# Kernel of four residual layers: rows of 528 columns instead of 514 for the split inputs of both convs

## The reference

```python
x = x + conv(x, W0, groups=4, taps=9, pad=4) + context + bias      # layer 0
x = x + agg_w1[b] @ x + agg_b1[b]                                  # layer 1
x = x + agg_w2[b] @ x + agg_b2[b]                                  # layer 2
x = x + conv(x, W3, groups=4, taps=9, pad=4) + context + bias      # layer 3
```

## Time and profile before

| | |
|---|---|
| median of 3 runs | 2578.09 us (2578.03 to 2578.33) |
| the profiled execution | 2577.78 us |
| its span, from the first to the last instruction | 2575.7 us |
| PE busy | 2550.1 us (99%), 11068 matmuls |
| weight loads (PEld, beside PE) | 2069.8 us (80%) |
| ACT busy | 2100.5 us (82%) |
| DVE busy | 1955.4 us (76%) |
| POOL busy | 16.1 us (1%) |
| DMA, mean over the span | 314 GB/s |
| granted TensorE clock, mean | 0.997 |

### The profile page before, as it was taken

The page is one execution under the profiler, slowest core; times in us unless marked ns, Lnnn a source line. Parts: engine busy times, 40 slices in busy tenths (PEclk is TensorE's granted clock), DMA queues, the critical chain, the costliest instruction groups (busy, mean ns, idle before and its releaser), DMA issues.

```text
span 2575.7 us, 42996 instructions
## 1 busy us (share of the span) xinstructions
PE 2550.1 (99%) x11068; PEld 2069.8 (80%) x11068; DVE 1955.4 (76%) x5032; ACT 2100.5 (82%) x1937; POOL 16.1 (1%) x29
## 2 busy tenths in 40 slices
PE   8999999999999999999999999999999999999998
PEld 6888888888888888888888888888888888888886
DVE  8777777777777777777777777777777777777774
ACT  6888888888888888888888888888888888888885
POOL 2000000000000000000000000000000000000000
PEclk9999999999999999999999999999999999999999
DMA  7888888888888888888888888888888888888876
GB/s 254 316 320 317 318 319 319 315 318 323 318 312 321 323 318 313 320 324 316 315 320 323 315 317 319 322 317 316 320 320 317 317 319 319 316 318 322 317 297 237
DMA packets 334986, 809.31 MB, mean 314 GB/s; under 512 B 37370, under 2 KB 39426, under 8 KB 302210
## 3 DMA queue, kind: packets, MB, share of 16 engines
q1 hardware_dynamic: 332736, 807.69, 84.3%
q10 hardware_dynamic: 2242, 1.53, 0.2%
HBM read 137.97 MB, written 134.23 MB: 106 GB/s over the span
## 4 chain that ended last, share of the span: by engine, by line
PE 98%; DMA 1%; DVE 1%; ACT 0%; SPq 0%; issue 0%; DVEq 0%; ACTq 0%
PE pair L877 82%; PE quad L927 14%; PE pair L917 1%; DMA x_ch<-x_ph 0%; DVE partial L701 0%; DMA mix<-att_saved 0%; DMA x_ph<-in_small 0%; SPq L269 0%; SPq L321 0%; SPq L294 0%; DMA att_saved<-att 0%; ACT x_out L569 0%; ACT x_ch L422 0%; DVE x_hi L734 0%; ACT x_ph L575 0%
## 5 line engine op out<-in xcount | busy, mean ns | idle before, releaser
L877 PE MATMUL pair<-x_hi,w_hi 128*128 128x512 f32 x3072 | 1227.7, 400 | 2.9 <-DVE x_lo L752 1.2
L877 PE MATMUL pair<-x_hi,w_lo 128*128 128x512 f32 x3072 | 1213.5, 395 | 0.0
L877 PE MATMUL pair<-x_lo,w_hi 128*128 128x512 f32 x3072 | 1209.2, 394 | 0.0
L877 PEld LDWEIGHTS pair<-x_hi,w_lo 128*128 128x128 f32 x3072 | 579.7, 189 | 137.5
L877 PEld LDWEIGHTS pair<-x_lo,w_hi 128*128 128x128 f32 x3072 | 582.0, 189 | 131.7
L877 PEld LDWEIGHTS pair<-x_hi,w_hi 128*128 128x128 f32 x3072 | 579.0, 188 | 131.3 <-DVE x_lo L752 1.6
L484 ACT ACTIVATE x_ph<-pair,bias_now 128x512 f32<-128x512 f32 x512 | 351.2, 686 | 254.8 <-PE pair L877 254.7
L422 ACT COPY x_ch<-x_in 128x1024 f32<-128x1024 f32 x255 | 528.3, 2072 | 0.0
L475 ACT COPY x_out<-x_ch 128x1024 f32<-128x1024 f32 x252 | 517.3, 2053 | 0.0
L493 ACT ACTIVATE x_ph<-pair,bias_now 128x512 f32<-128x512 f32 x508 | 355.5, 700 | 191.3 <-PE pair L877 191.3
L734 DVE CAST x_hi<-x_ch 128x512 fp32r<-128x512 f32 x512 | 204.9, 421 | 325.9 <-DMA x_ch<-x_ph 325.9
(11 more groups left out here) (83 smaller groups left out, 772.9 us busy)
## 6 DMA issues: line engine op xcount, KB each, us to landing
x_ph<-x_ch SPq DMA_DIRECT2D x1024, 256.0 KB, 2.5
x_ch<-x_ph SPq DMA_DIRECT2D x1024, 256.0 KB, 2.6
x_in<-in_x SPq DMA_DIRECT2D x128, 1024.0 KB, 5.6
out<-x_out SPq DMA_DIRECT2D x128, 1024.0 KB, 4.3
x_out<-in_W SPq DMA_DIRECT2D x8, 144.0 KB, 3.9
expert<-in_e ACTq DMA_DIRECT2D x2, 512.0 KB, 8.1
mix<-att_saved SPq DMA_DIRECT2D x2, 512.0 KB, 6.3
x_ph<-in_small ACTq DMA_DIRECT2D x1, 458.5 KB, 3.4
```

The source lines that it names most:

```text
L877: mm = nc.tensor.matmul(conv_bank[g % 2], w[l][:, m, g, :], x[:, g, m:m + N], start=(m == 0 and x is hi and w is w_hi), stop=(m == BLK - 1 ...
```

## The change

The rows of the four split inputs of the convs get 14 more columns, which nothing reads or writes. `ROW` = 512 + 16 = 528 columns are 2112 bytes, 33 x 64. The slices that are written and read keep their columns. Each of the four tensors grows from 8224 to 8448 bytes per partition, so x_lo begins at byte 57728 (902 x 64), x3_hi at 115328 (1802 x 64) and x3_lo at 123776 (1934 x 64); the tensors between x_lo and x3_hi stand 448 bytes further on, and those behind x3_lo 896 bytes. x_hi stays where it was. The instructions of every engine, their order and their waits are the same before and after, but for the addresses.

```diff
@@ -38,6 +38,7 @@
     HALO = BLK // 2
+    ROW = N + 16
     K = a["e0"].shape[0]
@@ -65,16 +66,16 @@
         x_ph = sb("x_ph", [C, G, N])
-        x_hi = sb("x_hi", [C, G, N + 2 * HALO], f32r)
-        x_lo = sb("x_lo", [C, G, N + 2 * HALO], f32r)
+        x_hi = sb("x_hi", [C, G, ROW], f32r)
+        x_lo = sb("x_lo", [C, G, ROW], f32r)
...
         x3_ph = sb("x3_ph", [C, G, N])
-        x3_hi = sb("x3_hi", [C, G, N + 2 * HALO], f32r)
-        x3_lo = sb("x3_lo", [C, G, N + 2 * HALO], f32r)
+        x3_hi = sb("x3_hi", [C, G, ROW], f32r)
+        x3_lo = sb("x3_lo", [C, G, ROW], f32r)
```

## The result

The changed kernel takes 2585.85 us in the median of 8 runs (2584.46 to 2587.25), the kernel before 2577.39 us in as many (2576.72 to 2578.33). The ratio is 1.0032, with a 95% interval of 1.0023 to 1.0042: 8.5 us slower. The forecast was 2586.4 us.

The account below looks back on a forecast made before the run. TensorE's back-to-back matmuls were taken to bound the kernel. 2577.8 - 0.2 (64 bytes) + 8.5 (16 bytes) = 2586.1 us, with 0.3 for the median 2586.4; range 2572 to 2594.

Parts of the forecast that it names:

- What bounds the kernel: Whole kernel: TensorE, busy 2550.1 of 2575.7 us; other engines matter only if they become late.
- the cover of conv4's first matmul: The third x1 group is evacuated 0.57 us before conv4, which waits for it, begins; cost 0.
- The 16 bytes: Conv matmuls, m = 1 of groups 1 and 3: offset 12 becomes 4, 0.017 us a triple, 512 triples, 8.5 us slower.
- The 64 bytes: Conv matmuls: starts at multiples of 64 go from 3 to 12 per 36, worth only 0.2 us.
- The other terms: VectorE and ScalarE work, tensors moved by 448 or 896 bytes, waits and halo fills: 0 in all.
- Rival 2: Timing depends on more of the address than its last 16 bytes, new places quick: 2563 or 2570 us; chance 0.12.
- Rival 1: Conv matmuls: the start does not matter, the pattern belongs to banks or weights; 2578 us, chance 0.31.
- Rivals 3 and 4: Conv starts beside 64 cost 19.3 ns each, 2534 us, chance 0.03; or conv4 waits for late moves, 2591 us, chance 0.03.

Follow-up runs that it names:

- the pitch alone: Rows of 528 columns, with 200 spare columns behind each split tensor keeping places modulo 1024 bytes, against the kernel before: 2584.47 us, ratio 1.0026.
- two columns on: The changed kernel with the data two columns further on in each row of 528: 2564.32 us, ratio 0.9951 to the kernel before.
- The kernel with one start per block: No layers: 2528 matmuls in blocks of 16, each block with one moving and one weight start, while x is copied; sixteen starts take 3.63 to 3.78 us.

## Why the prediction came out

**What bounds the kernel** was right: in the loop of none of these kernels does PE wait for another engine, and the cover of conv4's first matmul is still there, 0.58 us.

**The 16 bytes** were the right step, and most of the convs' time came from it: m = 1 of the odd groups went from 0.69 us to between 0.70 and 0.72. Forecast were 0.067 us a batch. At just these four triples the changed kernel takes 0.076 us more and the pitch alone 0.072, so this term was right in place and in size. What it left out is that the other places move too: in sum they cost 0.03 us more in the changed kernel, where the convs lose 0.11 in all, and 0.02 less with the pitch alone, where they lose 0.05; over many places it is 0.07. Also right was to trust the offset and not the PSUM bank: the same groups in the same banks speed up and slow down with the data's column, and with rows of 576 columns both banks show one pattern.

**The 64 bytes** buy nothing, as said; with not one start at 64, two columns on is 21 us quicker than the changed kernel. The argument for it was not sound, though. The middle product was taken as a yardstick for an aligned row, 232.5 ns, but it stood at a slow distance from its weights, and at a good one takes 2.72 / 12 = 226.7 ns.

**The other terms** hold the error, and two of the signs that the prediction named did not come: the conv piece was to be 16.82 us and is 16.86, the middle was to stay at 2.79 and fell to 2.74. Moving tensors by multiples of 64 was priced at 0. It gave the middle 0.05 us a batch, some 6 us of gain in all, and the convs some 0.05 of loss beyond what the pitch alone costs; the two nearly cancel. Had they had one sign, the forecast would have missed by more than 10 us. That the total came within 1 us is in this part luck. Rival 2 named this dependence (more of the address than its last 16 bytes) and expected it to be a gain; it was one for the middle only. Rival 1's time did not come, but the weights, which it named, do have a part in the pattern. Rivals 3 and 4 did not happen.

**What stays open.** Why 12 should be the cheapest offset and 4 the dearest is not explained; nor is how one spacing follows from the last ones in a changing sequence. The two effects were measured, not derived.

## What to carry to other kernels

Where TensorE's fp32r matmuls are back to back and nothing else is late, look at the starts in the trace by their place in the loop before touching a layout: here a fixed pattern of some nanoseconds came from addresses and not from contention. Aligning rows is no aim by itself; here the quicker layouts of the convs begin at 8, 12 and 0 bytes within 16, at both places of the weights that were tried, and the middle product, whose rows keep one start, is quickest with the weights at the same place modulo 256 bytes as the row. Change pitch and places apart, since padding one tensor moves all that follow, and their effects can hide each other.

## What was not expected of the hardware

A stream of equal matmuls is not evenly spaced: after some matmuls it mostly repeats a short pattern, and where that has one to three members its mean is 16, 18.7, 20, 21.3, 24, 26.7, 28, 29.3 or 32 cycles above 256, so that its sum is a multiple of 8 cycles of 1.2 GHz. The best, 226.7 ns for 512 columns, was never undercut in a block's steady state. The spacing seems to have a memory: conv1's changed when only the rows of the product before it were moved, and one distance can end in either of two patterns. Load of the DMA engines does not show in it. The kernel with one start per block meets distances 0 and 12 again behind the end of its copy, and takes 3.63 and 3.67 us there, as against 3.63 and 3.66 with the DMA engines at work (stretch, us, busy, granted clock, DMA share, GB/s):

```profile
549.73:553.36 3.63, 3.63 (x18) 1.00 0.00 0
586.96:590.63 3.67, 3.67 (x18) 1.00 0.00 0
```
